# A 66-column matmul for the upper probabilities in a two-layer cross-attention and FFN kernel, with a VectorE sum of its halves and new task orders

## The reference

```python
x = x + L0_xattn(layernorm(x), ctx)   # q, k l2-normalised over 512; out + Qp, then a layer norm
x = x + L0_ffn(layernorm(x))          # Hadamard, 4-bit levels, ternary weight
x = x + L1_xattn(layernorm(x), ctx)   # q, k not normalised, scores clipped at 1e4
x = x + L1_ffn(layernorm(x))          # 512 -> 2048 (ternary), exact gelu, 2048 -> 512 (ternary)
# both xattn: 16 heads of 32, out = softmax(q k^T * 32**-0.5) v, then a projection
```

## Time and profile before

| what | value |
|---|---|
| median of 3 runs | 1847.98 us (1845.79 to 1848.81) |
| profiled execution, own time | 1849.33 us |
| its span, first to last instruction | 1847.5 us |
| mean granted TensorE clock, share of full | 0.971 |
| instructions in the span | 45915 |
| TensorE matmuls | 18714 |

### The profile page before, as it was taken

The page is one execution under the profiler, slowest core; times in us unless marked ns, Lnnn a source line. Parts: engine busy times, 40 slices in busy tenths (PEclk is TensorE's granted clock), DMA queues, the critical chain, the costliest instruction groups (busy, mean ns, idle before and its releaser), DMA issues. The chain is left out here.

```text
span 1847.5 us, 45915 instructions
## 1 busy us (share of the span) xinstructions
PE 1732.0 (94%) x18714; PEld 1058.0 (57%) x18714; DVE 1221.6 (66%) x2454; ACT 1052.4 (57%) x1954; POOL 915.2 (50%) x1062
## 2 busy tenths in 40 slices
PE   5789999999999999999999999986779999999999
PEld 2455666666666666666666666664544444444443
DVE  5658778687786867878677786888953333334332
ACT  5675866868677586875868768563542222222221
POOL 1662846748466484754847557472452223222221
PEclk9789999999999999999999999989869999999999
DMA  7122020211202112021120202243320110011100
GB/s 235 35 92 75 11 96 2 96 56 42 95 2 96 42 56 95 2 96 41 57 95 2 96 19 79 90 161 112 126 70 6 46 46 36 11 46 46 46 24 23
DMA packets 46343, 115.56 MB, mean 63 GB/s; under 512 B 5420, under 2 KB 9644, under 8 KB 45112
## 3 DMA queue, kind: packets, MB, share of 16 engines
q1 hardware_dynamic: 43832, 104.25, 16.6%
q0 software_dynamic: 2304, 8.39, 1.1%
HBM read 72.78 MB, written 31.46 MB: 56 GB/s over the span
## 5 line engine op out<-in xcount | busy, mean ns | idle before, releaser
L759 POOL TENSOR_TENSOR arena<-arena 128x512 f16<-128x512 f32 x512 | 556.9, 1111 | 173.6 <-ACT arena L908 173.4
L900 ACT ACTIVATE arena<-psum 128x512 f32<-128x512 f32 x512 | 309.7, 612 | 65.4 <-PE psum L1445 32.1
L908 ACT ACTIVATE arena<-arena 128x512 f16<-128x512 f32 x512 | 329.0, 651 | 1.2 <-PE psum L1465 1.1
L956 ACT ACTIVATE arena<-psum,arena 128x512 f32<-128x512 f32 x128 | 88.1, 688 | 352.7 <-PE psum L1483 352.7
L1289 PE MATMUL psum<-arena 128*128 128x512 f16 x672 | 260.3, 387 | 7.8 <-ACT arena L900 4.0
L1290 PE MATMUL psum<-arena 128*128 128x512 f16 x672 | 258.0, 384 | 0.0
L1293 PE MATMUL psum<-arena 128*128 128x512 f16 x672 | 257.6, 383 | 0.0
L1483 PE MATMUL psum<-arena 128*128 128x512 f16 x1024 | 243.3, 380 | 1.4 <-DVE arena L1226 1.4
L789 POOL TENSOR_TENSOR arena<-arena 128x512 f16<-128x512 f32 x64 | 73.0, 1140 | 342.3 <-DVE arena L1233 342.3
L1493 PE MATMUL psum<-arena 128*128 128x512 f16 x1016 | 240.0, 378 | 1.2 <-POOL arena L789 1.2
L1233 DVE CAST arena<-arena 128x512 f16<-128x512 f32 x128 | 54.7, 427 | 272.0 <-ACT arena L956 271.8
(11 more groups left out here) (122 smaller groups left out, 3328.2 us busy)
## 6 DMA issues: line engine op xcount, KB each, us to landing
arena<-in_x SPq DMA_DIRECT2D x32, 512.0 KB, 4.5
arena<-x_scratch SPq DMA_DIRECT2D x32, 512.0 KB, 5.3
arena<-in_L_ffn_W SPq DMA_DIRECT2D x16, 1024.0 KB, 5.2
arena<-arena SPq DMA_DIRECT2D x16, 512.0 KB, 6.6
x_scratch<-arena POOLq DMA_DIRECT2D x16, 512.0 KB, 6.2
x_scratch<-arena SPq DMA_DIRECT2D x16, 512.0 KB, 3.0
out<-arena SPq DMA_DIRECT2D x14, 512.0 KB, 3.8
arena<-in_ctx SPq DMA_DIRECT2D x16, 384.0 KB, 5.5
```

The costliest lines, as they stand in the source:

```text
L759: gp.tensor_tensor(pl[l][:, h % NP, :], pf[l][:, h % NF, :], ph[l][:, h % NP, :], ALU.subtract).then_inc(p_lo[l].sem, 1)
L900: sc.activation(pf[l][:, h % NF, :], bank(u.bank), ACT.Exp, scale=SCALE / (QS * QS) if l == 0 else SCALE).then_inc(read[u.bank], 1)
L908: sc.activation(ph[l][:, h % NP, :], pf[l][:, h % NF, :], ACT.Copy).then_inc(p_hi[l].sem, 1)
```

## The change

- `attend`: in the first seven of a bank's eight slots the upper probabilities meet all 66 columns of `vs` in one matmul, into a slot of 66 (at a stride of 68); the lower probabilities add to its first 33 columns. The eighth slot, of 33 columns, keeps its three matmuls, for the bank has 512 columns. A slot then holds upper sums, the row sum, a second column of sums, and the part from the lower values.
- `attn_out`: after the reciprocal VectorE adds the two parts of the seven wide slots by a sum over pairs that lie 34 columns apart into a tile `osum` of 7 x 32, and multiplies 128 and 96 elements of it; the eighth slot has its own product of 32 elements. It waits for the previous call's bank in all calls, not within a layer only.
- `vs` gets rows of 68 (`VP`), of which 66 (`VW`) are used; `squared` goes, and the squares are written to the lower half of the row tile of `xn[0]`; `osum` takes its place.
- `ORDER` and `ORDERS` have new digits.

```diff
-VP = 66
+VW, VP = 66, 68
-ORDER = ("0021312111112210000002010100001110011011100131330003333101033333031133113113102113331133312322102323"
-         "13032123232321321313113031113033131012230120123303230222023222223232121320222020010121220011212")
+ORDER = ("0210111211213210120000000010101101001110113001130303313032130130213013333311131130333323123201132311"
+         "32133320122331233131123301101313031133201222033023123322201220332222222213200222120200011120211")
...
-        squared = take(D // 2).bitcast(BF16)
+        osum = take((NT * HG - 1) * HD).rearrange("p (i d) -> p i d", d=HD)
-        rden = [tiny(NT * HG).rearrange("p (t h) -> p t h", t=NT) for _ in range(2)]
+        rden = [tiny(NT * HG) for _ in range(2)]
...
+                        squared = xn[0][:, k, 0:D // 2].bitcast(BF16)
                         sc.activation(squared, (qf0, kf0)[j][:, k, :], ACT.Square,
...
+            outs = []
+
             def attn_out(l, b, g, use):
                 u = use["o", l, g]
-                if g:
-                    dve.wait_ge(read[use["o", l, g - 1].bank], use["o", l, g - 1].read_at)
+                for bank_n, read_at in outs[-1:]:
+                    dve.wait_ge(read[bank_n], read_at)
+                outs.append((u.bank, u.read_at))
                 dve.wait_ge(av_done[l].sem, av_done[l].at(b, (g + 1) * HG))
-                o = bank(u.bank)[:, 0:NT * HG * OW].rearrange("p (t h d) -> p t h d", t=NT, h=HG)
-                chain(v.reciprocal(rden[l], o[:, :, :, HD]))
+                slots = NT * HG - 1
+                o = bank(u.bank)
+                pairs = o[:, 0:slots * VP].rearrange("p (i s d) -> p i d s", s=2, d=VP // 2)
+                v.reciprocal(rden[l], o[:, HD:slots * VP + OW:VP]).then_inc(dve_step, 1)
+                chain.n += 1
+                chain(v.tensor_reduce(osum, pairs[:, :, 0:HD, :], AX_X, ALU.add))
                 dst = attn[l].rearrange("p t (h d) -> p t h d", h=H)[:, :, g * HG:(g + 1) * HG, :]
                 for k in range(NT):
-                    ins = v.tensor_tensor(dst[:, k], o[:, k, :, 0:HD], rden[l][:, k, :].unsqueeze(2).to_broadcast([P, HG, HD]), ALU.mult)
-                    if k == NT - 1:
-                        ins.then_inc(read[u.bank], 1)
+                    n = HG if k < NT - 1 else HG - 1
+                    v.tensor_tensor(dst[:, k, 0:n], osum[:, k * HG:k * HG + n],
+                                    rden[l][:, k * HG:k * HG + n].unsqueeze(2).to_broadcast([P, n, HD]), ALU.mult)
+                v.tensor_scalar(dst[:, NT - 1, HG - 1], o[:, slots * VP:slots * VP + HD], rden[l][:, slots:slots + 1], None,
+                                ALU.mult).then_inc(read[u.bank], 1)
...
-                    at = (q * HG + h % HG) * OW
-                    out = bank(u.bank)[:, at:at + OW]
+                    slot = q * HG + h % HG
+                    wide = slot < NT * HG - 1
+                    pair = bank(u.bank)[:, slot * VP:slot * VP + (VW if wide else OW)]
+                    out = pair[:, 0:OW]
                     for k in range(NT):
...
-                        te.matmul(out, p_hi_t, vs[l][:, k, h, 0:OW], start=(k == 0), stop=False)
-                        te.matmul(out[:, 0:HD], p_hi_t, vs[l][:, k, h, HD + 2:VP], start=False, stop=False)
-                        mm = te.matmul(out, p_lo_t, vs[l][:, k, h, 0:OW], start=False, stop=(k == NT - 1))
+                        if wide:
+                            te.matmul(pair, p_hi_t, vs[l][:, k, h, 0:VW], start=(k == 0), stop=(k == NT - 1), skip_group_check=True)
+                        else:
+                            te.matmul(out, p_hi_t, vs[l][:, k, h, 0:OW], start=(k == 0), stop=False)
+                            te.matmul(out[:, 0:HD], p_hi_t, vs[l][:, k, h, HD + 2:VW], start=False, stop=False)
+                        mm = te.matmul(out, p_lo_t, vs[l][:, k, h, 0:OW], start=False, stop=(k == NT - 1), skip_group_check=wide)
```

More of the change, by code:

```diff
@@ L73, in __call__ @@
         self.eng.wait_ge(self.sem, self.n)
-ORDER = ("0021312111112210000002010100001110011011100131330003333101033333031133113113102113331133312322102323"
-         "13032123232321321313113031113033131012230120123303230222023222223232121320222020010121220011212")
+ORDER = ("0210111211213210120000000010101101001110113001130303313032130130213013333311131130333323123201132311"
+         "32133320122331233131123301101313031133201222033023123322201220332222222213200222120200011120211")
 ORDERS = {
[L81 to L90, removed]
+    0: ("000400000000000404000000000000400040000000000000"),
+    1: ("0111111110111400111010000101000111001001010001011011001111001404440011110040400011111101141111011000"
+         "01111114410"),
+    2: ("2011112110122121110112010100001000011100110010000201110100110121021001221121101222022022201200220211"
+         "102122211212201102201121222210102221211101212"),
+    B: ("2311331311331311111331131433133333132423114221214312211133333323231321133131133311343131311213142223"
+         "2212212111131223213411322222412221232322342231232222221111111"),
+    B + 1: ("3323333334334323333234433343332332332334333232434223334243423234423432232243242423234423344223232443"
+         "2222222222222244222"),
+    B + 2: ("33333333333333333333333333333433333334334343333443333433443"),
 }
@@ L1083, in step @@
                             dve.wait_ge(v_hi[l].sem, v_hi[l].at(b, k + 1))
-                            v.scalar_tensor_tensor(out=vs[l][:, k, :, HD + 2:VP], in0=heads(bank(u.bank)), scalar=1.0 / WS,
+                            v.scalar_tensor_tensor(out=vs[l][:, k, :, HD + 2:VW], in0=heads(bank(u.bank)), scalar=1.0 / WS,
                                                    in1=vs[l][:, k, :, 0:HD], op0=ALU.mult,
```

## The result

The changed kernel takes 1901.1 us (median of 4, 1900.27 to 1903.6) against 1848.39: ratio 1.0288, 95% interval 1.0275 to 1.0300. It is 53 us slower, where 21 us faster was forecast.

What follows compares the result with a forecast made beforehand. TensorE was taken to set the pace, with VectorE second in an iteration's first stretch and ScalarE in its last. Savings of 22.9 and 1.2 us less 3 in the tail took 1849.3 to 1828.2, median 1827 us; range 1811 to 1843.

Steps and rivals of the forecast that it cites:

- term 2: VectorE's attention-output call: sum and split products add 0.55 us each time, 4.4 us an iteration, still under TensorE.
- The slower case: VectorE becomes the bound in the iteration's first stretch and the tail: 1883 us; chance 0.10.
- Term 4: New task orders: move no work in or out, cover the output transposes' 0.6 us wait, counted at nothing beyond this.
- Term 1: TensorE's attention matmuls: 66 columns at 29.5 ns replace a pair of 50.6, saving 2.36 us a full iteration.
- rival of 38.8 ns: Dearer wide matmul on TensorE: a slot saves only 11.8 ns, giving about 1837 us; chance 0.08.
- estimate of 45 ns: Wide matmul's price by the skill's spacing rule: 66 columns take about 45 ns, saving only 10 us in all.
- Term 3: ScalarE and GpSimd: work unchanged, but ScalarE's full last stretch loses 0.6 us of an iteration's saving.
- Term 2's cover: VectorE's 5.57 us idle in the iteration's first stretch takes the 2.2 us that four longer calls add.
- rival 2: ScalarE and VectorE keep the old pace, 0.6 us an iteration stay saved: 1843 us; chance 0.15.
- Term 5: Tail past 1200 us, where VectorE is about 87% busy: 16 longer calls fall there, taken as +3 us.

Runs made afterwards that it cites:

- e1: Changed kernel with the reciprocals written to free columns of the result's PSUM bank, so products read one SBUF and one PSUM operand: 1865.59 us, ratio 1.0091.
- e8: Changed kernel with GpSimd filling the probabilities' lower halves with zeros instead of subtracting, their part left out of the result: 1847.24 us in one run.
- e4: Kernel before with the new task orders alone, matmuls and attention output as before: 1869.75 us, ratio 1.0117.
- e11: e4 with layer 1's turned-context load issued ahead of layer 0's loads of x and context: 1862.41 us, ratio 1.0078.
- e15: e11 with layer 1's statistics and normalising moved back behind layer 0's heads in the full iterations: 1942.28 us, ratio 1.0508.
- e5: Changed kernel with the old orders and without VectorE's sum, the lower halves' part left out of the result: 1833.65 us, ratio 0.9932.
- e6: Kernel before with one added VectorE sum of 448 PSUM elements in each call, its result unused: 1863.12 us, ratio 1.0087.
- e9: e2 with the wide matmuls and VectorE's sum in layer 0 only, layer 1 as in the kernel before: 1859.33 us, ratio 1.0066.
- e10: e2 with the wide matmuls and VectorE's sum in layer 1 only, layer 0 as in the kernel before: 1844.57 us, ratio 0.9987.
- e2: e1 with the task orders of the kernel before: 1854.85 us, ratio 1.0038.

## Why the prediction was wrong

**The sum's products in term 2 are the step that failed most.** The prices of the "products of 128 and 96 elements, 0.20 and 0.17" were taken from the products of before, which read one operand from PSUM. The changed ones read both from SBUF. They took 586 and 563 ns on average, once 8.2 us; that is 35.5 us of the 53 (e1 against the changed kernel), and e8 shows that it hangs on GpSimd's reads. The slower case, to which 0.10 was given, had the right engine, but its mechanism (all calls at 0.55, or a slow sum) is not what happened. The trace of before had a row for it that I didn't use, the shortest, middle and longest of an instruction with two SBUF operands, against the product that reads PSUM:

```profile
L1150 DVE SCALAR_TENSOR_TENSOR arena<-arena x32: 721/762/1642, 81.1 to 1237.2; 128x512 f32<-128x512 f32 x32
...
L1206 DVE TENSOR_TENSOR arena<-psum,arena x256: 280/288/295, 57.7 to 1368.1; 128x128 f32<-128x128 f32 x128
```

One ranges from 721 to 1642 ns, the other from 280 to 295. Beside 556.9 us of GpSimd subtractions a spread like the first is a reason to look what the longest ones lie next to: in the packed trace each of the twelve longest starts within 10 ns of a subtraction, lies beside the whole of it, and ends 0.55 us behind it.

**Term 4, "I count the orders at nothing", failed:** 21.5 us (e4). The step that SyncE's loads keep their numbers was right, and overlooked what is queued ahead of them: the turned context stands behind the store of layer 1's output and two other loads. Taking the two loads away from ahead of it ends that wait and gives back a third of the cost (e11). The rest shows as waits for lower halves behind ScalarE; that it is the normalising moved into ScalarE's full stretch, as the text feared, stays open, since e15 tested something else.

**Term 1 was right in price and wrong in worth.** 29.5 ns was taken and 30.5 measured; the rival of 38.8 ns is out, and so is the estimate of 45 ns from the 81 ns of the Trainium skill (TensorE: Matmul & The Clock Gate, Back-to-back issue gap). But of 2.36 us an iteration (2.25 at the measured price) only 1.0 reached the time (e5), where 1.76 had been counted. Term 3 charged 0.6 us for ScalarE's full stretch; about 1.2 were lost, to that stretch and to the 0.13 us longer call together.

**Term 2's cover was wrong besides.** A call without the conflict is 0.62 us longer than before (1347 against 725 ns from the reciprocal's start to the last product's end, e1's trace and before's), a little more than the 0.55 taken. VectorE "still under TensorE" is an average. Eight sums of 0.57 us in an iteration make it 1.0 us longer (79.1 us in e6 against 78.1), in a kernel where VectorE is busy for 77% of it; and the layer whose heads lie where VectorE has most idle time is the one where the change loses (e9), not the other (e10). Without a conflict and with the old orders the change is 6.6 us slower (e2): rival 2, in which ScalarE and VectorE keep the old pace, was the nearest for that kernel and gave 1843; it measured 1855.

**Term 5:** with the conflict the tail is 23.2 us longer, without it 1.6 (e1), against +3 taken.

The sum in measured terms: +21.5 orders, -4.2 wide matmuls with the longer call under the new orders (e1 against e4), +35.5 conflict; 52.8 together. These are steps from one kernel to the next, so they add up by construction, and in another order they have other sizes: with the old orders the conflict is 89.9 and the wide matmuls with the longer call +6.6.

A version faster than both kernels exists, by little: wide matmuls in layer 1 only, with the reciprocals in PSUM and the old orders (e10), 0.9987 (0.9977 to 0.9996), some 2 to 3 us; the interval ends just below 1.

## What to carry to other kernels

Before pricing a VectorE instruction by its size, look where its operands lie: with two in SBUF beside a busy GpSimd, add the rest of the GpSimd instruction that may be under way (up to 1.1 us here, beside products of 0.29), and put one operand in PSUM if a free column is there. A saving on an engine that is 98% busy is worth only what its neighbours can follow, stretch by stretch, and an engine's idle time is no cover by itself: eight sums put into 18 us of VectorE's idle time in an iteration cost 1.0 us (e6). When an order is moved, follow each queue and ask what stands ahead of the load, not only what moved past it.

## What the runs showed of the hardware that was not expected

A VectorE product of two SBUF operands stood until the GpSimd subtraction under way was over, up to 1.2 us for a product of 0.25 to 0.29, and then mostly got in ahead of the next one; once it did not, and stood for 8.2 us, through eight subtractions. The other side hardly paid: a subtraction took 1124 ns on average instead of 1111. A GpSimd instruction that only writes (the filling of e8) left such products at their undisturbed length.
